# Routed experts on collected tokens: seven experts in ten passes of 256 rows instead of 512 tokens each

## The reference

```
top_vals, top_idx = jax.lax.top_k(logits, 2)          # logits = flat_x @ W_router + b_router, 8 experts
for e in range(8):
    expert_mask = jnp.any(top_idx == e, axis=-1)
    h = jax.nn.relu(flat_x @ W1[e] + b1[e])            # 256 -> 1024
    y = h @ W2[e] + b2[e]                              # 1024 -> 256
    w = router_weights[:, e] * expert_mask
    final_output = final_output + y * w[:, None]
```

## Time and profile before

| | us |
|---|---|
| median of 3 runs | 971.53 (970.67 to 972.51) |
| profiled execution, whole time | 974.7 |
| its span, first to last instruction | 972.9 |
| TensorE busy | 930.1 (96%) |
| VectorE busy | 733.4 (75%) |
| GpSimd busy | 557.7 (57%) |
| ScalarE busy | 502.7 (52%) |
| chain that ended last, TensorE's share | 85% |
| expert 1's first matmul | 810.94 |
| last matmul's record ends | 969.68 |

### The profile page before, as it was taken

How to read it: one execution, slowest core, us unless ns; L and a number is a source line. 1 busy time by engine, 2 the same in 40 slices (tenths; PEclk the granted TensorE clock), 3 DMA queues, 4 the chain that set the end, 5 groups by cost and what they waited for, 6 DMA issues and landing times.

```text
span 972.9 us, 16568 instructions
## 1 busy us (share of the span) xinstructions
PE 930.1 (96%) x6116; PEld 799.2 (82%) x6116; DVE 733.4 (75%) x1147; ACT 502.7 (52%) x856; POOL 557.7 (57%) x590
## 2 busy tenths in 40 slices
PE   6999999999999999999999999999997699999998
PEld 3568888888888888888888888888786587888887
DVE  5658787787977978778797787865776667888776
ACT  3556556665666555656566665664452333344332
POOL 5729678768948957876894895720000442444440
PEclk9999999999999999999999999999999799999999
DMA  5872112212211211221221121101005022222200
GB/s 161 284 243 62 45 57 59 63 42 60 64 38 52 71 39 58 58 63 40 59 67 39 52 70 37 56 4 65 1 2 173 11 85 78 87 87 88 87 1 22
DMA packets 75087, 66.42 MB, mean 68 GB/s; under 512 B 7920, under 2 KB 71680, under 8 KB 75008
## 3 DMA queue, kind: packets, MB, share of 16 engines
q1 hardware_dynamic: 75008, 65.37, 22.3%
HBM read 57.48 MB, written 7.86 MB: 67 GB/s over the span
## 4 chain that ended last, share of the span: by engine, by line
PE 85%; DVE 11%; ACT 3%; issue 1%; DMA 0%; SPq 0%; POOL 0%; DVEq 0%; ACTq 0%
PE sps L1194 28%; PE scp L1212 9%; PE scp L1214 9%; PE scp L1213 9%; PE scp L1409 5%; PE sps L1395 4%; PE wps L1395 4%; PE scp L1410 3%; DVE u_sb L910 2%; PE wps L1239 2%; DVE st L875 1%; PE sps L1307 1%; PE scp L1162 1%; PE sps L1148 1%; DVE pt_lo L900 1%
## 5 line engine op out<-in xcount | busy, mean ns | idle before, releaser
L1212 PE MATMUL scp<-cn,pt_hi 128*128 128x258 f32 (+1 forms) x832 | 240.0, 288 | 4.4 <-DVE pt_lo L900 3.7
L1213 PE MATMUL scp<-cn,pt_hi 128*128 128x256 f32 (+1 forms) x832 | 235.5, 283 | 0.0
L1214 PE MATMUL scp<-cn,pt_lo 128*128 128x258 f32 (+1 forms) x832 | 235.2, 283 | 0.0
L900 DVE TENSOR_TENSOR pt_lo<-st,pt_hi 128x512 fp32r<-128x512 f32 (+1 forms) x208 | 196.1, 943 | 6.8 <-ACT pt_hi L670 6.8
L661 ACT ACTIVATE st<-sps 128x512 f32<-128x512 f32 (+1 forms) x208 | 123.4, 593 | 149.1 <-PE sps L1194 148.2
L875 DVE TENSOR_TENSOR st<-st,mbc 128x512 f32<-128x512 f32 (+1 forms) x208 | 156.7, 754 | 38.9 <-ACT mbc L684 38.4
L1194 PE MATMUL sps<-qk_hi,ct_hi 128*128 128x512 f32 (+1 forms) x416 | 168.4, 405 | 11.3 <-DVE cmax L886 5.8
L667 ACT ACTIVATE st<-st 128x512 f32<-128x512 f32 (+1 forms) x208 | 130.3, 627 | 88.4 <-DVE st L875 87.8
L1212 PEld LDWEIGHTS scp<-cn,pt_hi 128*128 128x128 f32 (+1 forms) x832 | 157.3, 189 | 14.9 <-DVE pt_lo L900 6.6
L1194 PE MATMUL sps<-qk_hi,ct_lo 128*128 128x512 f32 (+1 forms) x416 | 164.4, 395 | 0.0
L1213 PEld LDWEIGHTS scp<-cn,pt_hi 128*128 128x128 f32 (+1 forms) x832 | 157.7, 190 | 7.5 <-issue 0.2
(11 more groups left out here) (209 smaller groups left out, 1447.6 us busy)
## 6 DMA issues: line engine op xcount, KB each, us to landing
w_raw<-W SPq DMA_DIRECT2D x16, 1024.0 KB, 7.5
raw<-ctx_t SPq DMA_DIRECT2D x96, 128.0 KB, 2.2
raw<-ctx_n SPq DMA_DIRECT2D x96, 128.0 KB, 2.0
raw<-qk_scratch SPq DMA_DIRECT2D x56, 128.0 KB, 2.0
qk_scratch<-stage_b SPq DMA_DIRECT2D x4, 896.0 KB, 4.8
qk_scratch<-stage_a SPq DMA_DIRECT2D x4, 896.0 KB, 4.6
wq_sb<-w_q SPq DMA_DIRECT2D x1, 1024.0 KB, 5.8
wkt_sb<-w_kt SPq DMA_DIRECT2D x1, 1024.0 KB, 8.3
```

Source lines behind the costliest of these rows:

```text
L900: dve.tensor_tensor(pt_lo[0:rows(j), r, :], st[0:rows(j), par, j, :], pt_hi[0:rows(j), r, :].bitcast(F32), ALU.subtract).then_inc(lo_ok, 1)
L1212: pe.matmul(scp[:, t, 0:D + 2], hi, cn[0:rows(j), j, 0:D + 2], start=j == 0, stop=False)
L1213: pe.matmul(scp[:, t, 0:D], hi, cn[0:rows(j), j, D + 2:CNW], start=False, stop=False)
L1214: ins = pe.matmul(scp[:, t, 0:D + 2], lo, cn[0:rows(j), j, 0:D + 2], start=False, stop=j == SJ - 1)
```

## The change

Experts 1 to 7 are no longer computed for every token.

- **Routing.** For each token and each of its two experts a slot number 512 x expert + rank is made: one-hot rows and their sum on VectorE (`cnt`), ranks by small matmuls with a triangular and an all-ones matrix on TensorE (`rank`, called in `first_ranks` and `last_rank`), then `routes` on VectorE for tiles 0 to 2 (a) and tile 3 (b). Nine small VectorE instructions find the experts with over 256 tokens.
- **Collecting.** GpSimd scatters the normed rows (`xln`) into `xg_scratch` in DRAM with eight indirect DMAs; both scratch tensors (2 x 4 MB) are first filled with zeros by four DMAs on SyncE's queue, `clear_rows`, put at slot 29 of the first pass.
- **Passes.** Ten passes z = 0 to 9 of 256 rows: experts 1 to 7 with their first 256 rows, then three passes for the rest, always run, with an expert number read on SyncE from `unit_i`. The pass works on unit z+1; there are 11 units of weights where there were 8. A pass loads its rows (`load_x`), transposes them on TensorE, splits them on ScalarE and VectorE (`take_xt`, `xt_low`), makes 8 h and 8 y tiles on 256 columns, and copies y out (`take_y` on ScalarE, `finish_y` on VectorE, `store_y` on SyncE).
- **Weights.** From unit 2 on GpSimd makes three low parts of four and VectorE the last (`low_weights` there).
- **End.** After the last store GpSimd gathers 2 x 4 tiles of rows with eight indirect DMAs and VectorE adds them to `x_sb` with the gates `tw2` (zero for expert 0, which stays dense).

```diff
+NOV = 3
+NZ = NE - 1 + NOV
+NU = NZ + 1
+ROWS = NE * TOK
+ZERO_AT = 2 * SJ + 3
...
+            def clear_rows():
+
+                sp.wait_ge(zero_ok, 1)
+                for dst in (xg_dram, yg_dram):
+                    n = ROWS // P
+                    v = dst.rearrange("(n p) d -> p n d", p=P)
+                    for h in range(DT):
+                        sp.dma_start(v[:, :, h * P:(h + 1) * P],
+                                     zrow[:].unsqueeze(1).broadcast_to((P, n, P))).then_inc(zeroed, 16)
+
...
                         qk_stored()
                         load_weights()
+                    if of == 0 and u == ZERO_AT:
+                        clear_rows()
                     for job in slot_jobs(of * PASS + u):
...
+            def load_x(z):
+                if z == 0:
+                    sp.wait_ge(scattered, 16 * 2 * MT)
+                if z >= 2:
+                    sp.wait_ge(xt_pe, z - 1)
+                sp.dma_start(xg_sb[:, z % 2, :, :],
+                             xg_dram[rows_of(z), :].rearrange("(a p) d -> p a d", p=P)).then_inc(xg_in[z % 2], 16)
+
+            def store_y(z):
+                sp.wait_ge(yb_ok, z + 1)
+                if z >= NE:
+                    sp.wait_ge(yg_out[(z - 1) % 2], 16 * ((z - 1) // 2 + 1))
+                sp.dma_start(yg_dram[rows_of(z), :].rearrange("(a p) d -> p a d", p=P),
+                             ybuf[:, z % 2, :, :]).then_inc(yg_out[z % 2], 16)
+
+            load_unit(0)
+            load_unit(1)
+            load_unit(2)
+            load_x(0)
+            load_x(1)
+            for z in range(NZ):
+                if z + 3 < NU:
+                    load_unit(z + 3)
+                if z + 2 < NZ:
+                    load_x(z + 2)
+                store_y(z)
             for m in range(MT):
-                sp.wait_ge(yc_ok, (NE - 1) * MT + m + 1)
+                sp.wait_ge(add_ok, 2 * (m + 1))
...
+            def scatter(m):
+
+                if m == 0:
+                    pool.wait_ge(zeroed, 16 * 2 * DT)
+                pool.wait_ge(route, ROUTE_NO["slot_b" if m == MT - 1 else "slot_a"])
+                pool.wait_ge(chain_dve[m], DVE_NO["ln2"])
+                for j in range(2):
+                    pool.indirect_dma_start(
+                        xg_dram, bass.IndirectOffsetOnAxis(slot_i[:, m, j:j + 1], 0),
+                        xln[:, m, :], None).then_inc(scattered, 16)
+
+            def gather(m):
+                for j in range(2):
+                    pool.indirect_dma_start(
+                        ytok[:, m, j, :], None, yg_dram,
+                        bass.IndirectOffsetOnAxis(slot_i[:, m, j:j + 1], 0)).then_inc(gathered[m], 16)
+
...
+            low_weights(1, 0)
             chain_rstd(3, 2)
-            for part in range(1, 4):
-                low_weights(0, 1, part)
-            for i in range(1, NE // 2):
-                for s in range(2):
-                    for part in range(4):
-                        low_weights(i, s, part)
+            for m in range(MT - 1):
+                scatter(m)
+            low_weights(1, 1)
+            scatter(MT - 1)
+            for part in range(2, 4):
+                low_weights(1, part)
+            for w in range(2, NU):
+                for part in range(3):
+                    low_weights(w, part)
+            for i in range(2):
+                pool.wait_ge(yg_out[i], 16 * (NZ // 2))
+            for m in range(MT):
+                gather(m)
 
 
...
+            def take_xt(z):
+
+                act.wait_ge(xt_pe, z + 1)
+                act.wait_ge(h_ok, FT * max(2, z + 1))
+                act.activation(xT_hi[:, z % 2, :, :], scp[:, 2 * (z % 2), :].rearrange("p (t q) -> p t q", t=DT),
+                               ACT.Copy).then_inc(xt_hi_ok, 1)
+
+            def take_y(z):
+
+                act.wait_ge(y_ok, unit_done(z + 1))
+                if z >= 2:
+                    act.wait_ge(yg_out[z % 2], 16 * (z // 2))
+                b0 = 2 * (z % 2)
+                act.activation(ybuf[:, z % 2, :, :], scp[:, b0:b0 + 2, 0:D], ACT.Copy).then_inc(ya_ok, 1)
...
+            for z in range(NZ):
+                if z == NE - 1:
+                    act.wait_ge(b1_in, 16 * NOV)
                 for f in range(FT):
-                    relu(i, s, i * 2 + (s + 1), f)
-                    if f % 2 and nxt:
-                        high_weights(*nxt, f // 2)
-
-            experts(0, 1, (1, 0))
-            for i in range(1, NE // 2 - 1):
-                experts(i, 0, (i, 1))
-                experts(i, 1, (i + 1, 0))
-            experts(NE // 2 - 1, 0, (NE // 2 - 1, 1))
-            experts(NE // 2 - 1, 1, None)
+                    relu_z(z, f)
+                    if f % 2 and z + 2 < NU:
+                        high_weights(z + 2, f // 2)
+                if z + 1 < NZ:
+                    take_xt(z + 1)
+                take_y(z)
 
 
...
+            def routes(m0, m1, x):
+
+                def after(name):
+                    dve.wait_ge(route, ROUTE_NO[f"{name}_{x}"])
+
+                n = m1 - m0
+                bank = (scp[:, 0, :] if m0 == 0 else hbank(2))[:, 0:n * NE].rearrange("p (m e) -> p m e", e=NE)
+                dve.wait_ge(rank_ok, 1 if m0 == 0 else 2)
+                dve.scalar_tensor_tensor(out=pos[:, m0:m1, :], in0=eidx[:].unsqueeze(1).broadcast_to((P, n, NE)),
+                                         scalar=float(TOK), in1=bank, op0=ALU.mult, op1=ALU.add).then_inc(route, 1)
+                after("pos")
+                dve.tensor_tensor(both[:, m0:m1, :, :], onehot[:, m0:m1, :, :],
+                                  pos[:, m0:m1, :].unsqueeze(2).broadcast_to((P, n, 2, NE)), ALU.mult).then_inc(route, 1)
+                after("both")
+                dve.tensor_reduce(slotf[:, m0:m1, :], both[:, m0:m1, :, :], AX.X, ALU.add).then_inc(route, 1)
+                after("sum")
...
+            def split_z(z, f):
+                p = z + 2
+                dve.wait_ge(hf_ok, p * FT + (f + 1))
+                dve.wait_ge(y_ok, p * FT + (f + 1 - FT))
+                dve.tensor_copy(h_hi[:, f, 0:TK], h_f[:, f % 2, 0:TK]).then_inc(hh_ok, 1)
+                dve.wait_ge(hh_ok, p * FT + (f + 1))
+                dve.tensor_tensor(h_lo[:, f, 0:TK], h_f[:, f % 2, 0:TK], h_hi[:, f, 0:TK].bitcast(F32),
+                                  ALU.subtract).then_inc(hl_ok, 1)
...
+            def finish_y(z):
+                b0 = 2 * (z % 2)
+                dve.wait_ge(ya_ok, z + 1)
+                dve.tensor_tensor(ybuf[:, z % 2, :, :], ybuf[:, z % 2, :, :], scp[:, b0:b0 + 2, D:2 * D],
+                                  ALU.add).then_inc(yb_ok, 1)
+
+            def low_weights(w):
+                raw_w, hi, lo = w_quarter(w % 2, 3)
+                dve.wait_ge(whi_ok, w * 4 + 4)
+                dve.tensor_tensor(lo, raw_w, hi.bitcast(F32), ALU.subtract).then_inc(w_last, 1)
+
+            xt_low(0)
+            for z in range(NZ):
                 for f in range(FT):
-                    split_h(i * 2 + (s + 1), f)
-                add_y(i, s, i * 2 + (s + 1), isinstance(i, int) and i * 2 + s == NE - 1)
-
-            expert(0, 1)
-            for i in range(1, NE // 2 - 1):
-                expert(i, 0)
-                expert(i, 1)
-            expert(NE // 2 - 1, 0)
-            expert(NE // 2 - 1, 1)
+                    split_z(z, f)
+                if z + 1 < NZ:
+                    xt_low(z + 1)
+                if z + 2 < NU:
+                    low_weights(z + 2)
+                finish_y(z)
+            dve.wait_ge(yc_ok, MT)
+            for m in range(MT):
+                dve.wait_ge(gathered[m], 32)
+                for j in range(2):
+                    if j == 1:
+                        dve.wait_ge(add_ok, 2 * m + 1)
+                    dve.scalar_tensor_tensor(out=x_sb[:, m, :], in0=ytok[:, m, j, :], scalar=tw2[:, m, j:j + 1],
+                                             in1=x_sb[:, m, :], op0=ALU.mult, op1=ALU.add).then_inc(add_ok, 1)
 
 
...
+            def rank(m):
+
+                bank = scp[:, 0, m * NE:(m + 1) * NE] if m < MT - 1 else hbank(2)[:, 0:NE]
+                for before in range(m):
+                    pe.matmul(bank, all_ones[:], cnt[:, before, :], start=before == 0, stop=False)
...
+            def transpose_x(z):
+
+                pe.wait_ge(xg_in[z % 2], 16 * (z // 2 + 1))
+                if z < 2:
+                    pe.wait_ge(yc_ok, 2 * (z + 1))
+                else:
+                    pe.wait_ge(yb_ok, z - 1)
+                for dt in range(DT):
+                    for a in range(2):
+                        n0 = (dt * 2 + a) * P
+                        ins = pe.transpose(scp[:, 2 * (z % 2), n0:n0 + P],
+                                           xg_sb[:, z % 2, a, dt * P:(dt + 1) * P], ident[:])
+                ins.then_inc(xt_pe, 1)
...
+                pe.wait_ge(hl_ok, (z + 2) * FT + (f + 1))
...
+            for z in range(NZ):
                 for f in range(FT):
```

(25 more changed lines are left out.)

233 lines of the change are left out of this document (185 added, 48 removed).

## The result

The changed kernel takes **1009.9 us** (median of 4 runs, 1007.0 to 1011.1), the kernel before 971.1; the ratio is 1.0395 (95% interval 1.0366 to 1.0423). Forecast were 1002 us and a range of 980 to 1027. The profiled execution's own time is 1008.9 us, its span 1007.2, against 974.7 and 972.9 before. (Of the experiments, one of e10's ten runs was slow, 1031.6 us at a granted clock of 0.85; it is in e10's median and not in its ratio.)

What follows compares the result with a forecast made beforehand. TensorE bounds the kernel before; in the shorter passes GpSimd's holds on VectorE would show. Passes -6.0, start +10, end +15.7, zeros +11 make +30.7, from 971.5 to 1002 us; 8-in-10 range 980 to 1027.

Steps and rivals of the forecast that it cites:

- What bounds the passes: In the passes, GpSimd's low weight parts hold VectorE's splits, so TensorE waits; 15.7 us a pass against its own 12.0.
- The length of a pass: 15.7 us for each of nine passes, 11.4 for the last: 152.7 against 158.7 before, -6.0 us.
- rival (C): TensorE's 2.7 us gap in each pass lowers the clock, 2.8 us more each time: 1015 or 1027 us; chance 0.17.
- the sum: All terms together, +30.7 us on the profiled run's 974.7; the same step from the median 971.5 gives 1002 us.
- Rival (A): Passes run at TensorE's own 12.0 us, -39.3: 969 us in all, 958 if the zeros are hidden too; chance 0.12.
- The zeros: Fills in SyncE's queue in the main loop delay the tiles behind them, at slots 35 and 39: +11 us.
- Rival (B): The zero fills do not delay the ring, as DMAs interleave or buffers cover them: 991 us; chance 0.13.
- The start of the passes: Between expert 0 and the first pass, rank matmuls, slot numbers, additions and row splits stand in line: +10 us.
- The end: After the last matmul, copy, store, eight gathers at 1.2 us each, additions and last store: +15.7 us.

Runs made afterwards that it cites:

- e10: The kernel before, with the low weight parts of experts 2 to 7 all on VectorE; 971.0 us, ratio 1.0002 to the kernel before.
- e2: The changed kernel with all low weight parts of units 2 to 10 on VectorE, none on GpSimd; 977.8 us.
- e3: The changed kernel with each of GpSimd's three low weight parts made in four instructions of 256 columns; 991.9 us.
- e8: The changed kernel with the fourth low weight part of units 2 to 10 on GpSimd too, none on VectorE; 1034.4 us.
- e4: The changed kernel with sixteen more 256-column matmuls in each pass, ahead of TensorE's wait for tile 6; 1002.5 us.
- e9: The changed kernel with the zeros filled as two blocks of 4.2 MB, the second 52 slots later; 999.2 us.
- e11: The changed kernel with unit 1's third and fourth low weight parts on GpSimd waiting for the first collected rows' low part; 1009.5 us.

## Why the prediction was off

The direction and the range held; the time was 7.9 us low. Step by step:

- **What bounds the passes.** Right: VectorE held still by GpSimd, at the two operations of tile 2 and at one of tile 6, TensorE waiting before y tiles 2 and 6. e2, e3 and e8 show the cause, not only the place. That the fourth part costs nothing on VectorE was right too: TensorE has no wait for it in a pass.
- **The length of a pass.** The term was mis-sized by two errors that nearly cancel. Undisturbed a pass is 14.9 us, not 15.7: a GpSimd part is 2.40 us here, where I took 2.6, from a row with VectorE operations twice as wide beside it (whether that is why was not tested); two of them back to back are 4.8 instead of 5.2. That made the pass too long. And the low clock, which I had as rival (C) and left out of the sum, is in five of the eight passes between transposes. That made it too short: five of the eight are 1.5 us longer than undisturbed. The mean is 15.85, near my 15.7 by luck as much as by working. With (C) at nothing I had 152.7 us for the ten passes, and they took 156.2: 3.5 us of the miss, 1.2 of them in these eight and the rest in the first pass (clock 0.78 in 832 to 839) and the last.
- **Rival (C).** Its mechanism came true, its price did not. I had 2.8 us for each such pass; it is 1.5, and 0.10 x 16.4 = 1.6 us by the granted clock of 0.90. It came in two passes and not in the third. e4 shows that the gap is the reason. The Trainium skill, "TensorE: Matmul & The Clock Gate", section "Part 1: The HAM clock gate", says that low speed is the default and activity lifts it. The traces agree: 0.90 in five of eight passes with the gap, 1.00 in all eight with e4's matmuls in it. It would have been right to put the rival and the forecast together: the forecast's own step makes the gap that (C) needs, so (C) was no alternative to it, but followed from it.
- **Rival (A)**, passes at 12.0 us, did not come; e2 comes near it with passes of 12.4 us, which is worth 32 us.
- **The zeros.** 11 forecast, 10.0 in the trace, 10.8 by e9's median. Right in place (slots 35 and 39) and in cause: slot 35's tile is split at 126.86 (127 forecast), slot 39 is 8.8 us late (9.6), and the clock is low for some us behind the stops. Rival (B) did not come; that the buffers cover the fills is true of a block half as large (e9). SyncE's own queue being stopped was not part of the step, and with the tile split on time it did not lengthen it.
- **The start of the passes.** +10 forecast, +11.6 measured, by the line on VectorE that the step lists. Two things in it I hadn't counted: the hold of 2.4 us in a cast, which e11 takes away without making the kernel faster, and the low clock of this stretch, whose price against full clock is open (a clock of 0.50 instead of 0.74 costs 3 us here). So the step's agreement may in part be luck.
- **The end.** +15.7 forecast, +15.9 measured; 1.2 us for an indirect DMA, 1.26 measured from one to the next. The estimate by the page "DMA: Bandwidth & Descriptors", section "Anatomy of one DMA", of the Trainium skill, for gathers one by one, some 7 us more, is not what happened. The landings follow each other at the 1.26 us of the issues, and only the last one (some 2.7 us) is paid, which is the overlap that the prediction read from that section.
- **From the trace to the median.** The sum was made on a profiled execution 3.2 us above its median and then put on the median. The change's profiled execution stands 1.0 us below its own. On like footing, own time against own time, 974.7 + 30.7 = 1005.4 was forecast and 1008.9 came, a miss of 3.5 us; the other 4.2 of 7.7 (1002.2 before rounding) are these two offsets, so more than half of the miss is no step of the working at all. The change's single runs lie between 1007.0 and 1011.1. Of the 3.2 us before, 2.8 are likely one stretch: from the last slot to expert 0 it is 111.7 us in the profiled run of before and 108.9 in e10's, with the same code there and a clock of 0.66 and 1.00 in 750 to 760.

## What to carry over

When a change makes a stage shorter for the bounding engine, the stage's other work keeps its length, and what was hidden can become the bound. List every hold and wait under the old cover and price each against the new length: the same edit is worth 0 us in e10 and 32 us in e2. A gap that such a hold makes on TensorE has a price of its own in the clock, 1.0 us a pass here. Of two engines that stop each other, give the shared work to the one that does it in half the time; cutting it into smaller pieces gives back only a part. And a bulk transfer in the queue that feeds the loop cost here only what exceeded the lead of the buffers, so cut it into pieces that fit: two halves did as well as 64 pieces.
